# Expert outputs of a routed layer added by the scattering DMA into two rows a token

## The reference

```python
def _L0_attn_ref(x, Wq, Wk, Wv, Wfc):
    ...
    scores = jnp.einsum('bshd,bstd->bsht', Q, K) / math.sqrt(hd)
    attn = jax.nn.softmax(scores, axis=-1)
    out = jnp.einsum('bsht,bstd->bshd', attn, V).reshape(b, s, dm)
    return out @ Wfc.T
...
topk_idx, topk_w = _route(tokens, router_weight, router_bias)
gate_vals = jax.nn.silu(jnp.einsum('th,eih->tei', tokens, gate_w))
up_vals = jnp.einsum('th,eih->tei', tokens, up_w)
expert_out = jnp.einsum('tei,ehi->teh', gate_vals * up_vals, down_w)
sel = jnp.take_along_axis(expert_out, topk_idx[:, :, None], axis=1)
mixed = (sel * topk_w[:, :, None]).sum(1)
...
x = _layernorm(x + _L0_attn_ref(x, Wq, Wk, Wv, Wfc), axis=-1)
x = _layernorm(x + _L0_ffn_ref(x, ...), axis=-1)      # mixed + shared
```

## Time and profile before

| | us |
|---|---|
| median of 3 runs | 721.03 |
| lowest and highest | 717.69, 722.21 |
| profiled execution, device time | 726.36 |
| its span, first to last instruction | 724.6 |

### The profile page before, as it was taken

How to read it: one execution, slowest core, us unless ns; L and a number is a source line. 1 busy time by engine, 2 the same in 40 slices (tenths; PEclk the granted TensorE clock), 3 DMA queues, 4 the chain that set the end, 5 groups by cost and what they waited for, 6 DMA issues and landing times.

```text
span 724.6 us, 16286 instructions
## 1 busy us (share of the span) xinstructions
PE 605.9 (84%) x4916; PEld 453.4 (63%) x4917; DVE 392.5 (54%) x1286; ACT 265.5 (37%) x521; POOL 290.1 (40%) x300
## 2 busy tenths in 40 slices
PE   6899998888597947578747989999999999993994
PEld 2366676565264625456524678788878888882883
DVE  2044675568056625368545446566565666562774
ACT  2344345334142502322212135455444555541224
POOL 4000003425327071516574316565556655554122
PEclk9999999789598977969776999999999999997899
DMA  6999968757237135859821224455445444444996
GB/s 225 270 223 250 238 187 236 174 163 214 99 109 220 45 126 181 323 180 382 286 106 67 90 71 148 133 144 157 147 133 154 150 159 158 148 153 153 417 411 238
DMA packets 125804, 135.34 MB, mean 187 GB/s; under 512 B 76856, under 2 KB 107071, under 8 KB 125120
## 3 DMA queue, kind: packets, MB, share of 16 engines
q1 hardware_dynamic: 108288, 95.92, 45.3%
q0 software_dynamic: 12672, 34.10, 12.5%
q10 hardware_dynamic: 4800, 4.74, 1.9%
HBM read 74.79 MB, written 60.96 MB: 187 GB/s over the span
## 4 chain that ended last, share of the span: by engine, by line
PE 15%; SPq 12%; issue 11%; DVE 6%; DMA 5%; another core or an unknown queue 2%; DVEq 1%; ACT 1%; POOL 0%; POOLq 0%; ACTq 0%
PE bank L868 14%; SPq L468 7%; SPq L470 5%; DMA wgu_sb<-pick_rows 3%; DMA prod<-expert_rows 2%; PE bank L1241 1%; DMA pick_rows<-prod,ids 1%; DVE prod L1709 1%; DVEq L250 0%; DVE prod L1733 0%; DVE bidx L1456 0%; DVE best L1453 0%; DVE gtop L1426 0%; SPq L474 0%
## 5 line engine op out<-in xcount | busy, mean ns | idle before, releaser
L527 POOL DMA_INDIRECT expert_rows<-stage,pos x128 | 127.2, 993 | 150.4 <-DVE pos L1393 80.4
L561 POOL DMA_INDIRECT pick_rows<-prod,ids x136 | 136.5, 1004 | 119.0 <-issue 51.8
L868 PE MATMUL bank<-prod 128*128 128x128 f32 x1088 | 134.4, 277 | 2.5 <-issue 1.3
L868 PEld LDWEIGHTS bank<-prod 128*128 128x128 f32 x1088 | 126.8, 192 | 5.7 <-issue 3.3
L868 PE MATMUL bank<-wgu_sb 128*32 128x64 f32 x2048 | 80.2, 297 | 50.3 <-issue 35.0
L868 PEld LDWEIGHTS bank<-wgu_sb 128*32 128x32 f32 x2048 | 64.5, 139 | 72.9 <-issue 59.2
L868 PE MATMUL bank<-wd_sb,wqkv_sb 128*128 128x512 f32 x192 | 92.8, 628 | 6.0 <-DMA wqkv_sb<-in_wqkv 6.0
L1709 DVE COPY prod<-wgu_sb 128x512 f32 x136 | 61.2, 491 | 63.0 <-issue 38.6
L827 ACT ACTIVATE prod<-bank,kept 128x256 f32<-128x256 f32 x136 | 57.1, 471 | 40.4 <-PE bank L868 21.9
L868 PE MATMUL bank<-wd_sb,prod 128*128 x272 | 70.3, 381 | 1.3 <-issue 0.8
L868 PEld LDWEIGHTS bank<-wd_sb,wqkv_sb 128*128 128x128 f32 x192 | 37.2, 201 | 46.3 <-issue 40.2
(11 more groups left out here) (138 smaller groups left out, 777.0 us busy)
## 6 DMA issues: line engine op xcount, KB each, us to landing
prod<-expert_rows SPq DMA_DIRECT2D x136, 132.0 KB
wgu_sb<-pick_rows SPq DMA_DIRECT2D x32, 512.0 KB, 14.1
wgu_sb<-in_wgu SPq DMA_DIRECT2D x2, 2560.0 KB
expert_rows<-pad_rows SPq DMA_DIRECT2D x4, 1056.0 KB
wd_sb<-in_xT SPq DMA_DIRECT2D x8, 512.0 KB, 4.3
q_slots<-wd_sb SPq DMA_DIRECT2D x16, 256.0 KB
k_slots<-wd_sb SPq DMA_DIRECT2D x16, 256.0 KB
wgu_sb<-q_slots SPq DMA_DIRECT2D x16, 256.0 KB
```

The source lines that it names most:

```text
L527: pool.indirect_dma_start(xs, bass.IndirectOffsetOnAxis(ap=pos[e % 2][:, i, k:k + 1], axis=0), stage[:, i, k, :], None, bounds_check=XROWS ...
L561: pool.indirect_dma_start(z, bass.IndirectOffsetOnAxis(ap=ids[par][:, j:j + 1], axis=0), y_sb[par][:, j, :], None, bounds_check=TOPK * NTO ...
L868: return pe.matmul(dst, lhsT, rhs, start=(k == 0), stop=(k == n - 1))
```

## The change

`pick_rows` (16,384 rows) becomes `pick_sums` with two rows a token and 256 rows for pads: 8448 rows. A label is now 2 * token, and `label_rows` adds j, so the output of a tile with j = 0 goes to the first row of its token and with j = 1 to the second. The scatter adds to what stands there. Because two scatters with the same j may meet in a row, each waits for the one ahead of it with the same j; semaphores `yscat0` and `yscat1` now stand for j instead of parity. The first set is taken out of the loop, so that the waits within it are for a positive count. The sums must start at zero: SP stores zeros over them in eleven parts of 768 KB (`clear_sums`), each behind a load of x or xT (parts 0 to 4 behind xT 3, xT 4, xT 5, x 2, x 3; 5 to 10 behind xT 6, x 4, xT 7, x 5, x 6, x 7). Pads are now written, to rows of their own. In the closing stage 32 loads of 256 KB go to eight buffers, DVE adds 256 columns a tile, and PE makes two matmuls instead of three. `ones_e` moves into a free part of `prod`.

```diff
-ZWAYS = 4
+SUMS = 2
+ZWAYS = 8
...
-NOWHERE = 1 << 18
+ZROWS = SUMS * (NTOK + P)
+ZERO_PARTS = 11
...
-    z = nc.dram_tensor("pick_rows", [TOPK * NTOK, DM], F32).ap()
+    z = nc.dram_tensor("pick_sums", [ZROWS, DM], F32).ap()
...
+            def clear_sums(part):
+                n = ZROWS // P // ZERO_PARTS
+                sp.dma_start(z.rearrange("(p r) c -> p r c", p=P)[:, part * n:(part + 1) * n, :],
+                             pad_rows[:, 0:DM].unsqueeze(1).broadcast_to([P, n, DM])).then_inc(S["z_zeros"], 16)
...
             sp.wait_ge(S["zeros"], 3)
+            sp.wait_ge(S["consts"], NCONST)
...
             load_xT(3)
+            clear_sums(0)
             write_q(2)
...
-                sp.wait_ge(y_scattered[par], quads * 32)
+                sp.wait_ge(y_summed[par], quads * 32)
...
-                if g >= ZWAYS:
-                    sp.wait_ge(S["d_ps"], TPC * (g - ZWAYS + 1))
...
-                for j in range(2):
+                for j in range(SUMS):
+                    if not (isinstance(pair, int) and pair * 2 + par == 0):
+                        wait_apart(pool, y_summed[j], (pair * 2 + par) * 16)
                     pool.indirect_dma_start(
                         z, bass.IndirectOffsetOnAxis(ap=ids[par][:, j:j + 1], axis=0),
-                        y_sb[par][:, j, :], None, bounds_check=TOPK * NTOK - 1,
-                        oob_is_err=False).then_inc(y_scattered[par], 16)
-
-            with pool.Fori(0, quads) as quad:
+                        y_sb[par][:, j, :], None, bounds_check=ZROWS - 1, oob_is_err=True,
+                        compute_op=ALU.add).then_inc(y_summed[j], 16)
+
+            pool.wait_ge(S["z_zeros"], 16 * ZERO_PARTS)
+            scatter_y(0, 0)
+            scatter_y(0, 1)
+            with pool.Fori(1, quads) as quad:
...
-                    act.wait_ge(y_scattered[par], old)
+                    for j in range(SUMS):
+                        act.wait_ge(y_summed[j], old)
...
-                    copy_y(n - 1, 1 - par, None if first else (quad * 32 if par else quad * 32 - 32))
+                    copy_y(n - 1, 1 - par, None if first else (quad * 32 - 16 if par else quad * 32 - 32))
...
-                    mm(to, ident[:, :], sx[:, at:at + DM], 0, 3)
-                    for k in range(2):
-                        last = mm(to, ident[:, :], zt[g % ZWAYS][:, t, k, :], k + 1, 3)
-                    last.then_inc(S["d_ps"], 1)
+                    mm(to, ident[:, :], sx[:, at:at + DM], 0, 2)
+                    mm(to, ident[:, :], zt[g % ZWAYS][:, t, 0, :], 1, 2).then_inc(S["d_ps"], 1)
...
-                    dve.wait_ge(y_scattered[par], old)
-                dve.tensor_copy(ids[par][:, :], kept[par][:, :, 0]).then_inc(S["ids_ready"], 1)
+                    for j in range(SUMS):
+                        dve.wait_ge(y_summed[j], old)
+                dve.tensor_tensor(ids[par][:, :], kept[par][:, :, 0], sum_of[:, :], ALU.add)\
+                    .then_inc(S["ids_ready"], 1)
...
-                    dve.tensor_tensor(zt[g % ZWAYS][:, t, 0:2, :], zt[g % ZWAYS][:, t, 0:2, :],
-                                      zt[g % ZWAYS][:, t, 2:4, :], ALU.add).then_inc(S["d_a"], 1)
+                    dve.tensor_tensor(zt[g % ZWAYS][:, t, 0, :], zt[g % ZWAYS][:, t, 0, :],
+                                      zt[g % ZWAYS][:, t, 1, :], ALU.add).then_inc(S["d_a"], 1)
```

More of the change, by code:

```diff
@@ L54 @@
 assert CH == 8
-NOWHERE = 1 << 18
+ZROWS = SUMS * (NTOK + P)
+ZERO_PARTS = 11
+assert ZROWS % (P * ZERO_PARTS) == 0
 assert MAXTILES + QUAD <= SLOTS
@@ L178, in build @@
         tend = sb("tend", [P, NE])
-        ones_e = sb("ones_e", [P, NE])
+        ones_e = over(prod, 25 * DM - NE, NE)
         past = sb("past", [P, 2, NE])
@@ L193, in build @@
         quadf = sb("quadf", [P, 1], U32)
+        sum_of = sb("sum_of", [P, SUMS])
         ids = [sb(f"ids{i}", [P, 2], U32) for i in range(2)]
@@ L204, in build @@
         ws = [over(prod, 8 * DM + 4 * ROW + 8 * P + i * 2 * KC * 2 * EI, 2, KC * 2 * EI) for i in range(2)]
-        zt = [over(wgu_sb, i * TPC * TOPK * DM, TPC * TOPK, DM).rearrange("p (t k) c -> p t k c", k=TOPK)
+        zt = [over(wgu_sb, i * TPC * SUMS * DM, TPC * SUMS, DM).rearrange("p (t k) c -> p t k c", k=SUMS)
               for i in range(ZWAYS)]
@@ L220, in build @@
         xt0 xt1 cX_ps cX_copied cmeta kept ws_ready ids_ready cgu_ps cth_ready cgth_ready ch_ready cy_ps cy_copied
-        yscat0 yscat1
+        yscat0 yscat1 z_zeros pair_base
         d_a d_ps dst_ready dmv_ready dveps_ready drstd_ready dnm_ready o2_ready stored0 stored1""".split()
@@ L227, in build @@
         xt_loaded = [S["xt0"], S["xt1"]]
-        y_scattered = [S["yscat0"], S["yscat1"]]
+        y_summed = [S["yscat0"], S["yscat1"]]
         z_loaded = [[sem(f"z_loaded{i}_{t}") for t in range(TPC)] for i in range(ZWAYS)]
@@ L361, in _ @@
             load_xT(4)
+            clear_sums(1)
             write_v(2)
@@ L375, in _ @@
             load_xT(5)
+            clear_sums(2)
             write_v(3)
@@ L382, in _ @@
             load_x(2)
+            clear_sums(3)
             read_k(3, range(3, 4))
@@ L385, in _ @@
             load_x(3)
+            clear_sums(4)
             read_v(3)
@@ L395, in _ @@
             load_xT(6)
+            clear_sums(5)
             read_o(2)
@@ L406, in _ @@
             load_x(4)
+            clear_sums(6)
             read_k(5, range(3, 4))
             load_xT(7)
+            clear_sums(7)
             write_q(6)
@@ L416, in _ @@
             load_x(5)
+            clear_sums(8)
             read_k(6, range(3, 4))
@@ L423, in _ @@
             load_x(6)
+            clear_sums(9)
             read_q(7)
             load_x(7)
+            clear_sums(10)
             write_k(7)
@@ L487, in _ @@
                     sp.dma_start(zt[g % ZWAYS][:, t, :, :],
-                                 z.rearrange("(n k) c -> n k c", k=TOPK)[at:at + P, :, :])\
+                                 z.rearrange("(n k) c -> n k c", k=SUMS)[at:at + P, :, :])\
                         .then_inc(z_loaded[g % ZWAYS][t], 16)
@@ L503, in _ @@
                       allow_small_or_imprecise_dtypes=True).then_inc(S["consts"], 1)
-            pool.iota(outid[:, :, :], [[P * TOPK, TPC], [1, TOPK]], base=0, channel_multiplier=TOPK,
+            pool.iota(outid[:, :, :], [[P * SUMS, TPC], [0, TOPK]], base=0, channel_multiplier=SUMS,
                       allow_small_or_imprecise_dtypes=True).then_inc(S["consts"], 1)
@@ L513, in _ @@
                                base=0, pattern=[[1, P]], channel_multiplier=-1).then_inc(S["consts"], 1)
-            pool.iota(pad_rows[:, ID:ID + 1], [[0, 1]], base=NOWHERE, channel_multiplier=1,
+            pool.iota(sum_of[:, :], [[1, SUMS]], base=0, channel_multiplier=0,
+                      allow_small_or_imprecise_dtypes=True).then_inc(S["pair_base"], 1)
+            pool.iota(pad_rows[:, ID:ID + 1], [[0, 1]], base=SUMS * NTOK, channel_multiplier=SUMS,
                       allow_small_or_imprecise_dtypes=True).then_inc(S["consts"], 1)
@@ L1299, in _ @@
             dve.wait_ge(S["bits"], 2)
+            dve.wait_ge(S["pair_base"], 1)
             dve.tensor_scalar(lower[:, :], lower[:, :], 0.0, None, ALU.is_gt).then_inc(S["masks"], 1)
@@ L1479, in route @@
                                              op0=ALU.mult, op1=ALU.mult).then_inc(S["idw_ready"], 1)
-                    dve.tensor_scalar(idw[:, :, :, 0], outid[:, :, :], float(b * CT * TOPK), None, ALU.add)\
+                    dve.tensor_scalar(idw[:, :, :, 0], outid[:, :, :], float(b * CT * SUMS), None, ALU.add)\
                         .then_inc(S["idw_ready"], 1)
@@ L1743, in pairs @@
                     first = isinstance(n, int) and n < 3
-                    label_rows(n - 1, 1 - par, None if first else (quad * 32 if par else quad * 32 - 32))
+                    label_rows(n - 1, 1 - par, None if first else (quad * 32 - 16 if par else quad * 32 - 32))
             copy_meta(0, 0, 0)
```

## The result

The changed kernel took 819.3 us (median of four runs, 812.7 to 823.5) against 720.3 us before: a ratio of 1.137, with a 95% interval of 1.128 to 1.145. It is slower, by 99 us. The profiled execution of the changed kernel happens to be its fastest run (812.66 us, span 810.9), and that of the kernel before is slower (726.36, span 724.6) than every run behind its median, so their spans differ by only 86 us.

A forecast was written before the change was run, and what follows sets the result against it. Three limits were named: mixed up to about 430 us, TensorE with its handshakes in the expert loop, memory traffic in the closing stage. Loop +65, closing stage -17, clears +4 gave +52 on 721, so 773 us; range 722 to 832.

The forecast's parts named there:

- the likeliest case: Expert loop: waits between same-j scatters make a set take 4.1 to 4.8 us, whole 753 to 800 us; chance 0.45.
- rival 4: Expert loop: a dear add, instruction 1.45 us, read 1.1 us, 5.2 us a set, whole 827 us (800 to 860); chance 0.14.
- The accumulate ... I take 0.8: Scatter landing in the loop: reading the destination before writing adds 0.8 us, bounds 0 and 1.8.
- Contention: Scatter landing in the loop: competing loads of expert rows add 0.45 us, between 0 and 1.2.
- Release to start: Expert loop: from a landing to the start of the next scatter in its chain, 0.82 us.
- GpSimd's own work ... stays under 3.43: Expert loop: GpSimd's two scatters at 1.28 us plus two short waits stay under 3.43 us a set.
- Rival 2: Expert loop: the add costs only a second move of 0.35 us, 3.96 us a set, whole 743 us; chance 0.22.
- Rival 3: Expert loop: waits hide in GpSimd's idle 1 us, only the closing stage and clears count, whole 708 us; chance 0.12.
- The closing stage: After the loop: less reloading, adding and matmul work, 42.9 us at 4.0 us a chunk, gain 17 us (12 to 20).
- The clears: Ahead of the loop: eleven stores of zeros, 24 us in all, mostly hidden, cost +4 us (0 to 24).
- rival 5: Attention: all 24 us of the clears exposed, beside the forecast's loop, whole 793 us; chance 0.03.
- The clock: Expert loop: TensorE's granted clock stays at 1.00 with TensorE about 74% busy.

The follow-up runs named there:

- e5: The kernel before, unchanged, run again on the 720 us kind of chip: 717.8 us, ratio 0.997.
- e6: The changed kernel, unchanged, run again on the 720 us kind of chip: 814.7 us against 720.2, ratio 1.132.
- e7: The changed kernel with all eleven clears moved behind the last load of weights on SP's queue: 808.2 us, ratio 1.122.
- e9: The changed kernel, unchanged, on the 635 us kind of chip: 741.4 us against 634.8 for the kernel before, ratio 1.168, one run.
- e12: The kernel of e7 once more, on the 720 us kind of chip: 809.4 us, ratio 1.123.
- e2: The kernel before with adding scatters, no waits between them, four rows a token cleared in 16 parts of 1 MB: 694.8 us against 637.9, ratio 1.089.
- e1: The changed kernel with the add taken off the scatter, waits and clears kept: 651.3 us against 637.9 for the kernel before, ratio 1.020.
- e8: The changed kernel with one chain instead of two, each scatter waiting for the one ahead whatever its j: 1123.2 us, one run.
- e11: The changed kernel with scatters of 64 of the 128 rows: 684.3 us against 634.8 for the kernel before, one run.
- e10: The changed kernel with scatters that add 128 of a row's 256 columns: 707.3 us against 634.8 for the kernel before, one run.
- e4: The kernel before with the changed kernel's closing stage, two picks a token left out: 620.9 us against 637.9, ratio 0.973.
- run 64: Not a run's name: the text reads "in the same run 64 such matmuls take about 2 us", 64 counting matmuls in e5.

## Why the prediction was right or wrong

The direction, the place and the mechanism were right: the loop becomes a chain of landings, two in parallel, and the closing stage gives back only part. The size was not. The forecast had +52 us, about half of the measured 99, and the likeliest case (4.1 to 4.8 us a set, 753 to 800 us) didn't hold the result. The range to 832 held the 819.3, but it is 110 us wide and reaches so far only for the sake of rival 4, so that was partly luck.

- **Sum.** Forecast +65 - 17 + 4 = +52 us. Measured in the profiled executions +99 - 16 + 3 = +86, in e5 and e6 +106 - 16 + 3 = +93. By medians it is +99 in the result and +94 in e6. The one term that was badly off is the loop's.
- **The step that failed** is "The accumulate ... I take 0.8". At the quiet end the landing is 3.62 against 2.34: the add costs 1.28 us (3.62 is the shortest last landing of five executions of such a chain; e6, e7, e9 and e12 have 3.73 to 3.82). 0.58 of it is GpSimd's instruction (0.975 to 1.556), 0.7 the DMA engines (0.35 to 1.07). I had one more move of 0.35 and 0.45 for both a read's latency and a longer instruction. My upper bound of 1.8 held; the argument that put me under half of it, that issue is already paid, was wrong, since the issuing itself grows.
- **The other terms of the landing held.** Contention was taken at 0.45: the mean landing of 4.04 less 3.62 is 0.42. Release to start was taken at 0.82: the mean is 0.83. With the right price for the add, 2.34 + 0.45 + 1.28 + 0.82 = 4.89 us a set; measured 4.90. That the two agree to a hundredth is chance, since e6 and e9 have 4.99 and 4.98.
- **A second floor that I ruled out.** "GpSimd's own work ... stays under 3.43" was reckoned with the plain instruction. With the adding one it is 3.83 us a set (e2). It isn't what ends last in the changed kernel, but without the chain it would hold the loop.
- **Rival 4, the dear add** (chance 0.14, instruction 1.45, 5.2 us a set, 827 us, 800 to 860), is what happened, with a longer instruction (1.556) and a cheaper read (0.7 where it had 1.1). It should have had a larger chance.
- **Rival 2** and its rule: the Trainium skill's "Collectives: The Full Stack", section "The bandwidth ceiling: the fold count and why AG ≠ RS ≠ AR", has an add in the DMA path run at half the rate of a copy, since it needs two source reads. The rows show about three times the engines' time instead of two, and besides it a longer instruction of GpSimd, of which that rule says nothing. The measurement decides.
- **Rival 3** needed landings of at most 2.6 us. Even plain ones are longer in the loop: in e1 they took 2.75 us on average, and a set 3.62.
- **The closing stage** came at 42.7 us against 42.9. A chunk was 3.66 and not 4.0 us: once under way DVE waits for no load any more, so the pace is that of TensorE and DVE and not of memory. A slower first chunk (statistics 7.6 us behind the first load) took the difference back, so the close agreement is partly luck.
- **The clears**: +3 where the forecast had +4, on that kind of chip (about 6 us by e6 against e7 and e12). My "about half should hide" was luck: on the other kind they cost 14 to 16 us. Perhaps they hide where the attention is held up by something else (last section); no run shows that. The bound of 24 us held on both, and rival 5, which had all of it exposed, fell.
- **The clock** didn't stay at 1.00 in the loop as I had said, but fell to a mean of 0.96. It cost nothing that shows: landing and release add up to the period without it, and still do in e8, at 0.69.

## What to carry to other kernels

An adding scatter is not a scatter with a free add: here it kept GpSimd 1.6 times and the DMA engines three times as long, and landed 1.3 us later. Where adds into one place must wait for each other, the period of a chain is landing plus release, and it has to be set against the loop's present period before anything else; one chain took 9.5 us a set and two took 4.99 (more weren't tried), but the issuing engine's instructions add up regardless. A saving in a short closing stage (17 us, once) is easily outweighed by 0.4 us in a step that runs 67 times.

## What the runs showed of the hardware that was not expected

- The adding scatter's instruction costs 1.40 us for 64 rows and 1.55 for 128: 64 rows more cost only 0.15 us.
- The adding scatter also makes more packets of the same bytes. The page's line for the queue of GpSimd's DMAs (packets, MB, share of the engines), before and after:

```profile
q0 software_dynamic: 12672, 34.10, 12.5%
```

```profile
q0 software_dynamic: 25728, 35.14, 24.1%
```

The extra 1.04 MB are the 1024 pad rows, which e1 writes too, with 12,672 packets. So an add on 128 rows takes 13,056 / 136 = 96 packets more than a plain scatter. With 64 rows (e11, 17,024 packets) each scatter has 64 fewer: one packet for each row. The number doesn't set the time alone, since e10 has the same 25,728 packets with half the bytes and lands sooner.
- Chips of two kinds: 635 to 638 us and 718 to 721 us for the same kernel before. The loop is the same (3.40 and 3.42 us a set), the closing stage too; the 80 us lie ahead of the loop. From 120 to 280 us (the same time, not the same work), on the fast kind (e4) and on the slow (e5), in the columns of the earlier trace rows:

```profile
120.00:280.00 160.00, 147.96 (x1591) 103.79 (x1583) 128.57 (x454) 66.91 (x114) 99.30 (x97) 0.98 0.80 260
```

```profile
120.00:280.00 160.00, 122.09 (x1166) 78.42 (x1157) 82.69 (x296) 48.12 (x81) 67.78 (x68) 0.81 0.49 145
```

On the slow kind there are stretches in which TensorE starts one to five short matmuls every 0.7 to 1.4 us and idles between with nothing that the profile names ("issue"). In e5 such stretches lie at 123 to 132, 148 to 151, 176 to 193 and 256 to 277 us, some 50 us together; elsewhere in the same run 64 such matmuls take about 2 us. The kernel before, e6, e7 and e12, all on this kind, have such stretches too; the runs on the fast kind (e1 to e4, e9 to e11) have none. At 181 us for instance:

```profile
181.25 0.38 PE L868 MATMUL bank<-wgu_sb 128*32 128x64 f32 x2 [1.08 <-issue]
...
183.40 0.27 PE L868 MATMUL bank<-wgu_sb 128*32 128x64 f32 x1 [0.35 <-issue]
```

What holds it there wasn't tried.
- A change's price differs with the kind: the same clears cost 3 to 6 us on one and 14 to 16 us on the other, and the same change has a ratio of 1.132 (e6) on one and, in one run, 1.168 (e9) on the other.
